# Moving the routed experts between attention's third and fourth batch, and the second layer's preparation into attention's last batches

## What is computed

```python
x = L0_attn_x                                  # (8, 512, 128)
xn = _layernorm(x)
s = attention(xn)     # softmax over 512 keys of 0.5 + 0.2 sigmoid(qk) + 0.15 tanh(qk) + 0.1 relu(qk)
g = _silu(moe(xn))    # xn + routed expert (1 of 8, by argmax) + shared expert
x = x + s * g
xn = _layernorm(x)
s = mamba(xn)         # causal conv of 4 taps, selective scan over 512 steps, 16 states, 256 channels
g = _silu(ffn(xn))    # silu-gated, 384 hidden
x = x + s * g
```

## Time and profile before

| | |
|---|---|
| median of the runs | 755.07 us |
| profiled execution, span | 756.3 us |
| PE busy | 670.0 us (89%) |
| DVE busy | 646.4 us (85%) |
| ACT busy | 502.3 us (66%) |
| POOL busy | 491.8 us (65%) |

### The profile page before, as it was taken

How to read it: one execution, slowest core, us unless ns; L and a number is a source line. 1 busy time by engine, 2 the same in 40 slices (tenths; PEclk the granted TensorE clock), 3 DMA queues, 4 the chain that set the end, 5 groups by cost and what they waited for, 6 DMA issues and landing times. The chain is left out here.

```text
span 756.3 us, 12992 instructions
## 1 busy us (share of the span) xinstructions
PE 670.0 (89%) x4010; PEld 491.6 (65%) x4010; DVE 646.4 (85%) x1105; ACT 502.3 (66%) x1023; POOL 491.8 (65%) x306
## 2 busy tenths in 40 slices
PE   1898999999799997869998998998999999988785
PEld 0865555556565553447776887787778777768765
DVE  5968877777567656889999999999999999999997
ACT  1665666666444443878879779788788797796453
POOL 1002652000054455076999999999999999999995
PEclk9999999999999998989999999999999999999999
DMA  7900110001222217435525335336146055154000
GB/s 201 293 1 14 39 38 22 0 0 28 59 69 70 71 47 94 123 140 166 124 80 136 108 114 120 91 114 172 38 140 155 32 167 153 67 139 118 1 15 15
DMA packets 43226, 67.56 MB, mean 89 GB/s; under 512 B 6296, under 2 KB 30368, under 8 KB 43168
## 3 DMA queue, kind: packets, MB, share of 16 engines
q1 hardware_dynamic: 31888, 48.42, 20.3%
q0 software_dynamic: 9552, 17.85, 11.6%
q10 hardware_dynamic: 1728, 0.57, 0.3%
HBM read 46.08 MB, written 9.74 MB: 74 GB/s over the span
## 5 line engine op out<-in xcount | busy, mean ns | idle before, releaser
L1709 DVE TENSOR_TENSOR_SCAN xnT_all<-psum,nfT_all 128x1024 f32<-128x1024 f32 x128 | 288.5, 2276 | 0.1
L1259 PEld LDWEIGHTS psum<-W_out,xnT_all 128*128 128x128 f32 x2048 | 237.3, 193 | 56.9 <-issue 54.3
L1259 PE MATMUL psum<-W_out,xnT_all 128*128 128x128 f32 x2048 | 242.7, 277 | 29.5 <-DVE acc L1725 27.4
L1432 ACT ACTIVATE psum<-delta,A 128x511 f32<-128x511 f32 x256 | 165.0, 683 | 59.9 <-DVE xnT_all L1709 59.8
L1239 POOL TENSOR_TENSOR nfT_all<-nf_rows,du 128x1024 f32<-128x1024 f32 x63 | 147.1, 2358 | 24.6 <-DVE nfT_all L1791 24.0
L1239 POOL TENSOR_TENSOR nfT_all<-attn_all,du 128x1024 f32<-128x1024 f32 x64 | 158.2, 2623 | 1.3 <-DVE xnT_all L1709 1.3
L570 POOL DMA_INDIRECT moe_dram<-xnT_all x40 | 38.8, 969 | 121.5 <-ACT xnT_all L826 121.5
L1725 DVE SCALAR_TENSOR_TENSOR acc<-psum,Cc,acc 128x128 f32<-128x128 f32 x284 | 78.0, 339 | 6.1 <-PE psum L1259 6.1
L559 POOL DMA_INDIRECT xs_dram<-nf_rows,pos x32 | 33.2, 1039 | 74.9 <-DVE pos L880 55.6
L1259 PE MATMUL psum<-vo_all,W_taps 128*128 128x512 f32 (+3 forms) x128 | 59.6, 613 | 0.7 <-ACT vo_all L1464 0.7
L1483 ACT ACTIVATE ts<-psum,Cc 128x128 f32<-128x128 f32 x188 | 52.8, 360 | 4.1 <-PE psum L1259 4.1
(11 more groups left out here) (218 smaller groups left out, 1131.8 us busy)
## 6 DMA issues: line engine op xcount, KB each, us to landing
nf_rows<-bt_dram SPq DMA_DIRECT2D x32, 512.0 KB, 4.8
attn_all<-bt_dram SPq DMA_DIRECT2D x32, 512.0 KB, 3.9
delta<-rl POOLq DMA_DIRECT2D x7, 512.0 KB, 7.0
e<-ab POOLq DMA_DIRECT2D x7, 512.0 KB, 5.6
delta<-e POOLq DMA_DIRECT2D x7, 512.0 KB, 6.5
xs_dram<-attn_all SPq DMA_DIRECT2D x4, 645.0 KB, 8.0
xnT_all<-xs_dram SPq DMA_DIRECT2D x40, 64.5 KB
x_all<-in_x_dram SPq DMA_DIRECT2D x8, 256.0 KB, 6.0
```

The source lines that it names most:

```text
L1259: return nc.tensor.matmul(o, l, r, start=start, stop=stop)
L1432: ins = nc.scalar.activation(dA[:, i % RA, k, 1:L], delta[:, p, h, 1:L], ACT.Exp, scale=A[:, h, 2 * q + k:2 * q + k + 1])
L1709: nc.vector.tensor_tensor_scan(hring[:, i % R, :, :].rearrange("p n l -> p (n l)"), dA[:, i % RA, :, :].rearrange("p n l -> p (n l)"), dbx ...
```

## The change

- The experts no longer follow attention's eighth batch. Batches 0 to 2 run first (`FIRST = 3`), the third without a successor (`more` is false); then the 40 slot tiles; then batches 3 to 7, which begin anew with `queries_keys(FIRST)`. Rounds are written out, no longer a loop. Attention's buffers move into one tensor `work` that outlives layer 0 and is reused by the mamba stretch; ts and the first three normalised batches lie in res_all.
- Scattering waits for the group of four before the last one, no longer for the last one; the slot loads wait for all scatters. PE's first turned slot tile needs such a load.
- Batches 3 to 7 add the gathered expert rows in their own `residual`.
- The gate is z(1 + tanh(z/2)), the half folded into the value weights: ACT makes the tanh (`gates`), POOL four operations of 128x512 for each batch (`gated`), the last of them onto x_all. DVE takes the statistics.
- `first_preparation(b, s)` puts pieces of the seam at four places s of rounds 4 to 7, in each engine's list. They all use bank 7, in turn with `shared_down`.
- What stays behind the last round: the decays, the last gate, `x_in` of batch 1, and in the first mamba round the last `gated`, the statistics of batch 7 and the norm of group (3 to 7).

The three batches, then the experts (PE; ACT and DVE alike), and the scatters on POOL:

```diff
-            with pe.Fori(0, NB - 1) as b:
-                round_(b, True)
-            round_(NB - 1, False)
+            for b in range(FIRST):
+                round_(b, b + 1 < FIRST)
...
-                if i % TPB == TPB - 1:
-                    pool.wait_ge(s_sc, (i + 1) * 16)
+                if i % TPB == TPB - 1 and i > TPB:
+                    g = i // TPB - 1
+                    pool.wait_ge(s_sc[g % 2], 16 * TPB * (g // 2 + 1))
```

The gate's part on POOL:

```diff
+                    g = gt[:, i % 2, :]
+                    pool.wait_ge(F["si"], i + 1)
+                    nc.gpsimd.tensor_tensor(g, g, rows_of(res_all), ALU.mult).then_inc(F["gs"], 1)
+                    pool.wait_ge(F["gs"], 2 * i + 1)
+                    nc.gpsimd.tensor_tensor(g, g, rows_of(res_all), ALU.add).then_inc(F["gs"], 1)
+                    pool.wait_ge(F["gs"], 2 * i + 2)
+                    pool.wait_ge(S["attn"], at(i, "attn", 1))
+                    nc.gpsimd.tensor_tensor(g, g, rows_of(attn_all), ALU.mult).then_inc(F["sg"], 1)
+                    pool.wait_ge(F["sg"], i + 1)
+                    nc.gpsimd.tensor_tensor(rows_of(x_all), rows_of(x_all), g, ALU.add).then_inc(F["x1"], 1)
```

PE's pieces; after those shown come W_x (FIRST + 2, 3), the first W_dt and turn(2) (FIRST + 3, 0 and 1), the second W_dt (3), skip and C (FIRST + 4, 0 and 1), then a wait for C's copy (2). Behind the last round stands x_in of batch 1:

```diff
+                    if (b, s) == (FIRST + 1, 1):
+                        pe.wait_ge(S["res"], at(b - 1, "res", 1))
+                        turn(0)
+                    elif (b, s) == (FIRST + 1, 2):
+                        pe.wait_ge(F["xT"], 1)
+                    elif (b, s) == (FIRST + 1, 3):
+                        pe.wait_ge(S["res"], at(b, "res", 1))
+                        first_in(0)
+                    elif (b, s) == (FIRST + 2, 0):
+                        pe.wait_ge(M["xv"], at6(0, "xv", 1))
+                        first_in(1)
+                    elif (b, s) == (FIRST + 2, 1):
+                        pe.wait_ge(M["xv"], at6(0, "xv", KH))
+                        turn(1)
...
+                pe.wait_ge(S["attn"], at(NB - 1, "attn", 1))
+                pe.wait_ge(S["shh"], at(NB - 1, "shh", KI))
+                x_in(1, 0)
+                x_in(1, 1)
```

ACT's pieces:

```diff
+                    if (b, s) == (FIRST, 3):
+                        gates(0)
+                        gates(1)
+                    elif (b, s) == (FIRST + 1, 0):
+                        gates(2)
+                        roots(0)
+                    elif (b, s) == (FIRST + 1, 1):
+                        turned(0)
+                    elif (b, s) == (FIRST + 1, 3):
+                        gates(3)
+                        conv_silu(0, 0)
+                    elif (b, s) == (FIRST + 2, 0):
+                        roots(1)
+                        conv_silu(0, 1)
...
+                    elif (b, s) == (FIRST + 4, 0):
+                        gates(6)
+                        w("acc_ps", 1)
+                        nc.scalar.activation(skip_sb[0], o.rearrange("p (j d) -> p j d", d=D), ACT.Copy)\
+                            .then_inc(M["acc0"], 1)
+                        w("ey", 1)
+                        nc.scalar.activation(lg[:, :, :], ab[:, :, :], ACT.Ln, bias=1.0).then_inc(M["lg"], 1)
+                        nc.scalar.activation(e1[:, :, :], ab[:, :, :], ACT.Identity, bias=1.0).then_inc(M["e1"], 1)
```

DVE's pieces:

```diff
+                    elif (b, s) == (FIRST + 1, 0):
+                        statistics(0)
+                        moments(0)
+                    elif (b, s) == (FIRST + 1, 2):
+                        norms(0)
+                    elif (b, s) == (FIRST + 2, 0):
+                        conv_gate(0)
+                        statistics(1)
+                        statistics(2)
+                        moments(1)
+                    elif (b, s) == (FIRST + 2, 2):
+                        conv_gate(1)
+                        norms(1)
...
+                    elif (b, s) == (FIRST + 4, 3):
+                        w("lg", 1)
+                        w("rl", KH)
+                        nc.vector.tensor_tensor(lg[:, :, :], lg[:, :, :], rl[:, :, :], ALU.add).then_inc(M["sp"], 1)
...
+                        nc.vector.tensor_tensor(du[:, 0, :, :], delta[:, 0, :, :], xv[:, :, :], ALU.mult)\
+                            .then_inc(M["du"], 1)
```

## The result

| | before | changed |
|---|---|---|
| median of the runs, same chip | 755.61 us (4 runs) | 786.58 us (4 runs) |
| ratio | | 1.0385, 95% interval 1.0352 to 1.0418 |
| profiled execution, span | 756.3 us | 783.5 us |
| mean granted clock | 0.981 | 0.967 |
| PE, DVE busy | 670.0, 646.4 us | 668.7, 639.0 us |

The change makes the kernel 31.0 us slower. The forecast was +14.9: the direction held and the waits that were counted came, the size did not. The two profiled executions are 27.2 us apart. The changed kernel's own was its fastest run, 785.32, which is 1.8 over its span and 1.3 under its median; with the same 1.8 that of before was some 2.5 over its median.

The account below looks back on a forecast made before the run. Bounds: PE in attention rounds, DVE in scans, the seam's 49.9 us running alone between. Second scan +12.9 and first mamba round +2.0 made +14.9: 771.2 us profiled, 770.0 median; 8-in-10 range 748 to 778.

Parts of the forecast that it names:

- step 5: Rounds from mark 3 to mark 7 with preparation pieces in them: 104.6 us, of which 20.8 us PE waiting.
- step 7: Matmuls at half clock behind long PE waits: 1.7 us at each of four and a half places, 7.7 us.
- step 8: First mamba round: +2.0 us for DVE's last-group work; ACT's root taken as hidden under two scans, bound +2.9.
- 1, 2: first slot tile: Three batches, then scatters gating the experts' start: first slot tile on PE at 115.8 us, cost 4.2 us.
- 3: experts: From first slot tile to last expert result: 80.0 us, as before the change.
- 4: restart to mark 3: Attention begun anew at batch 3 with nothing beside PE: 18.4 us to its mark, bounds 16.8 and 22.
- 6: behind mark 7: From the last round's mark to the second scan, with x_in of batch 1: 17.0 us.
- A: Rival for the whole kernel: the waits stand as counted, 770 us, range 762 to 778; chance 0.60.
- B: Rival: half of the waiting and clock cost is absorbed by PE's and DVE's slack, 755.8 us; chance 0.20.
- C: Rival: pieces are ready when PE comes to them, waiting and clock cost fall away, 741.5 us; chance 0.14.
- D: Rival: scatters keep drains, or ACT's root is not hidden, and POOL's gate is slower beside DVE, 780 us; chance 0.06.
- my 2.8 us: Batch 4's x_all later by this if POOL's four gate operations each met one DVE lock of 0.69; total 772.8 us.

Follow-up runs that it names:

- e6_four: Changed kernel with the preparation pieces behind the last round and the experts behind four batches instead of three: 785.41 us, ratio 1.0395.
- e3_onepool: Changed kernel with three of POOL's four gate operations per batch left out, so it does not compute the function: 776.96 us, ratio 1.0263.
- e9_dve_gate: e7_retimed with batches 0 to 6's gate on DVE, two batches' statistics in the first mamba round, and e8_root_early's root: 761.38 us, ratio 1.0052.
- e4_shifts: Changed kernel with DVE's reciprocal and shift of the last group one pair of scans later in the first mamba round: 790.73 us, ratio 1.0454.
- e11_last_gate: e10_four with the last batch's gate as three DVE operations behind the fourth scan instead of four on POOL: 761.50 us, ratio 1.0056.
- e13_warm_fit: Changed kernel with 6 and 7 unread matmuls filling PE's two waits of round 4, none in round 5: 781.49 us, ratio 1.0332.
- e8_root_early: Changed kernel with the last group's root on ACT directly behind the first mamba round's logarithm, shift as tensor_tensor: 781.47 us, ratio 1.0342.
- e7_retimed: Changed kernel with every preparation piece at another place in the rounds, nothing left out: 770.60 us, ratio 1.0174.
- e10_four: e9_dve_gate with the experts behind four batches instead of three: 756.26 us, ratio 0.9999 to the kernel before.
- e14_no_pool: e10_four with the last two batches' gates on DVE at places where POOL idles: 753.56 us, ratio 0.9958 to the kernel before.
- e2_early: Changed kernel with batch 0's gate, statistics and root one round earlier and its norm ahead of attended: 775.58 us, ratio 1.0250.

## Why the prediction was wrong, step by step

The sum was +14.9; the traces are +27.2 apart, 12.3 more. Three terms of the sum failed: step 5 left out that POOL holds up DVE (4.1 us), step 7 had the clock too small (by over 4), step 8 took a root as hidden that was not (2.6). The other 1.9 us lie ahead of the first mark.

| step | expected | trace | what it was |
|---|---|---|---|
| 1, 2: first slot tile | 115.8 | 117.50 | right: from the first mark 44.3 expected, 44.1 measured, 44.0 to 44.5 in eleven kernels with three batches ahead |
| 3: experts | 80.0 | 82.4 | +2.4, of which 1.8 are cold first products; e6_four shows 80.1 without the wait |
| 4: restart to mark 3 | 18.4 | 18.35 | right |
| 5: rounds | 104.6 | 116.4 | +11.8: 4.1 stretching in round 4, the rest clock |
| 6: behind mark 7 | 17.0 | 18.6 | +1.6, x_in of batch 1 cold (8.67 instead of 7.0) |
| 7: clock | 7.7 | in 3, 5, 6 | about 12 in all |
| 8: first mamba round | +2.0 | +4.6 | ACT's root not hidden |

**Direction and rival.** A's mechanism held: the norm behind the third theta made PE wait 6.3 (4.5 expected) in round 4 and 5.8 (5.4) in round 5, ACT's copy 3.1 in round 7. B and C are refuted by the marks: nothing was absorbed. D, held at 0.06, came nearest: ACT's root was not hidden, and POOL beside DVE cost time. But D had POOL slower, not DVE, and 780.

**Step 5 failed in round 4, on a resource I had priced on the wrong side.** I read in the earlier trace rows that POOL's operations keep their 1.27 us beside DVE, and took that for a sign that neither loses much; my 2.8 us let x_all come late. But x_all came on time, and DVE was held: 0.99 and 1.07 in the moments, 0.98 in W, 0.95 in the norm, 0.1 in the first difference, 4.1 us, all on PE's path. e3_onepool took it away, e9_dve_gate did so with the work kept, e4_shifts and e11_last_gate brought it about anew. The earlier trace rows could not have shown it: those POOL operations do not lose, and in those rounds DVE's heavy operations read PSUM. The Trainium skill ("SBUF — State Buffer", section "SBUF: two separate sides") has it as a lock for a whole instruction; round 4's ends, 231.60 at 231.57 and 232.93 at 232.91, agree with that, and e4_shifts shows that it can last several. By that section, which names tensor_scalar too, I should have counted every such DVE operation beside a gate, not one in each gate, and counted it against DVE.

**Step 7, the clock, was 7.7 and came out near 12.** Round 4 costs 3.65 (e13_warm_fit). Round 5's cold matmuls are 1.09, 1.92, 1.91 and 1.78 us instead of 0.6, 1.16, 1.02 and 1.02, 2.9 in all, which is also all that this round has over its 30.7. For these two rounds I had counted three places of 1.7: two to four matmul groups stand cold behind a wait, not one. In round 7 `shared_down` is cold:

```profile
331.11 3.75 PE L580 MATMUL psum<-shdown,work 128*128 128x128 f32 x16 [0.66 <-ACT Cc L1743]
```

It takes 1.95 us at full clock, so 1.8 here. With 1.7 in step 6 and 1.8 to 2.4 behind the first slot tile, a wait that step 2 had without any clock behind it, that is 11.9 to 12.5. Only round 4's part is tested by a run of its own; the others are differences of rows. Step 5 then closes to 0.7 us: 104.6 + 4.1 + 3.65 + 2.9 + 1.8 = 117.1, measured 116.4. Round 6 came out right (20.9 expected, 21.14 measured) in part by a slip: its own terms, 17.63 + 3.2 + 0.6, add up to 21.4.

**Step 8 had the price in its bound and took zero.** The root's table load starts at 378.90, behind two longer jobs, and DVE waits 3.52 us. e8_root_early gives 3.7 us back.

**What the change is worth when its costs are mended.** Order (e7_retimed), engine and early root (e9_dve_gate, e8_root_early), scatters (e10_four) and the last gates (e14_no_pool) together bring 33 us. Left is +3.9 us in the first mamba round, and e14_no_pool's trace has it in DVE's list: statistics of three batches and the moments of the last group 3.4, its reciprocal and shift 1.45 (the shift takes 1.23 us beside POOL's drive), less some 0.9, mostly because DVE waits less for PE there (0.74 instead of 1.56 us).

## What to carry to other kernels

Before work is put on POOL beside a busy DVE, list which DVE operations there have both inputs, or their one input and scalars, in SBUF, and count a POOL operation's length (in e4_shifts it was three of them) for each that is on the path; a stretch whose DVE operations read PSUM says nothing about it. Behind a wait of PE like those here (3.1 to 6.3 us), price the next two to four matmul groups at half speed, not one. And when a piece is moved earlier, look first at what its producer does on its own engine: here a root's two table loads put two waits of 2 us into PE's list (e2_early).

## What was not expected of the hardware

- DVE operations of 4 and 20 columns took 1.16 to 1.24 and 6.93 us beside POOL, and four norm operations of 128x128 took 4.75, 4.72, 4.25 and 2.06 instead of 1.11. POOL's own took 1.26 to 1.30, a few 1.60, one 1.80 and one 2.31 (e2_early, beside POOL's own issue of a transfer). Statistics out of SBUF (0.87 beside POOL) and operations with a PSUM input were not held.
- DVE did not get in between two POOL operations that follow closely (6.93 us over three of them), though in round 4 it did in a gap of 0.08 us.
- PE idled for 3.1 to 5.4 us ahead of the first slot tile in all kernels with three batches ahead, and for 0.5 at most with four.
